# Order of the adjacency products within a tile: bank by bank, three products each

## The reference

```
x, adj                     # 10000 x 128, 10000 x 10000
u = max(layernorm(x), 0)
h = item_feat @ W_item.T + b_item        # 10000 x 128
b = u @ W_user.T + b_user
out = x + relu(adj @ h + b)
```

## Time and profile before

| | us |
|---|---|
| median of 3 runs | 1154.68 |
| lowest, highest | 1153.7, 1154.87 |
| the profiled execution, its own time | 1155.03 |
| its span, first to last instruction | 1153.5 |
| TensorE busy | 1132.1 |
| VectorE busy | 976.4 |
| ScalarE busy | 773.4 |

### The profile page before, as it was taken

The page is one execution under the profiler, slowest core; times in us unless marked ns, Lnnn a source line. Parts: engine busy times, 40 slices in busy tenths (PEclk is TensorE's granted clock), DMA queues, the critical chain, the costliest instruction groups (busy, mean ns, idle before and its releaser), DMA issues.

```text
span 1153.5 us, 14338 instructions
## 1 busy us (share of the span) xinstructions
PE 1132.1 (98%) x5078; PEld 925.8 (80%) x5078; DVE 976.4 (85%) x683; ACT 773.4 (67%) x502; POOL 20.3 (2%) x42
## 2 busy tenths in 40 slices
PE   6999999999999999999999999999999999999998
PEld 5888888878888888788888887888888878888886
DVE  5989988888888888898898888888888888888886
ACT  4766767667676666576667675766666657667663
POOL 0000000000000000000000000000000000000000
PEclk9999999999999999999999999999999999999999
DMA  9999999999999999999999998999999999999993
GB/s 355 397 400 359 352 364 372 347 362 345 376 372 360 367 365 392 365 370 368 355 367 362 385 379 338 376 362 373 357 371 380 381 331 378 376 358 353 364 387 120
DMA packets 62659, 416.38 MB, mean 361 GB/s; under 512 B 7644, under 2 KB 9124, under 8 KB 62608
## 3 DMA queue, kind: packets, MB, share of 16 engines
q1 hardware_dynamic: 59984, 406.38, 92.3%
q0 software_dynamic: 2624, 9.22, 2.3%
HBM read 410.45 MB, written 5.12 MB: 360 GB/s over the span
## 4 chain that ended last, share of the span: by engine, by line
PE 96%; DVE 1%; issue 1%; ACT 1%; DMA 1%; DVEq 0%; SPq 0%; ACTq 0%
PE acc L508 61%; PE acc L514 31%; PE spare L464 2%; PE acc L497 1%; DVE y L397 1%; PE spare L490 1%; PE spare L484 1%; ACT hi_ring L277 1%; DMA items<-in_item_t 1%; DVE lo_ring L340 0%; PE acc L525 0%; DVEq L94 0%; DVEq L427 0%; SPq L199 0%; SPq L188 0%
## 5 line engine op out<-in xcount | busy, mean ns | idle before, releaser
L340 DVE TENSOR_TENSOR lo_ring<-a_ring,hi_ring 128x2000 fp32r<-128x2000 f32 x390 | 871.3, 2241 | 152.8 <-ACT hi_ring L277 151.4
L277 ACT CAST hi_ring<-a_ring 128x2000 fp32r<-128x2000 f32 x390 | 729.0, 1869 | 360.6 <-PE acc L514 357.2
L508 PE MATMUL acc<-hi_ring,h_lo 128*128 128x500 f32 x1560 | 434.6, 399 | 5.5 <-DVE y L397 4.4
L508 PE MATMUL acc<-hi_ring,h_hi 128*128 128x500 f32 x1560 | 420.0, 391 | 0.0
L514 PE MATMUL acc<-lo_ring,h_hi 128*128 128x500 f32 x1560 | 419.1, 390 | 0.0
L508 PEld LDWEIGHTS acc<-hi_ring,h_lo 128*128 128x128 f32 x1560 | 289.5, 189 | 76.4 <-DVE y L397 12.4
L514 PEld LDWEIGHTS acc<-lo_ring,h_hi 128*128 128x128 f32 x1560 | 294.2, 189 | 62.1
L508 PEld LDWEIGHTS acc<-hi_ring,h_hi 128*128 128x128 f32 x1560 | 293.9, 188 | 61.7
L464 PE MATMUL spare<-wi,items 128*128 128x128 f32 x156 | 23.9, 294 | 10.5 <-DMA items<-in_item_t 8.7
L464 PEld LDWEIGHTS spare<-wi,items 128*128 128x128 f32 x156 | 23.0, 206 | 12.9 <-issue 6.8
L345 DVE TENSOR_TENSOR h_full<-spare,bi 128x384 f32<-128x384 f32 x26 | 14.3, 551 | 10.3 <-DMA bi<-in_b_item_rows 6.6
(11 more groups left out here) (29 smaller groups left out, 113.8 us busy)
## 6 DMA issues: line engine op xcount, KB each, us to landing
a_ring<-in_adj_tiles SPq DMA_DIRECT2D x390, 1000.0 KB, 6.9
rows<-in_x_rows POOLq DMA_DIRECT2D x20, 250.0 KB, 7.6
items<-in_item_t SPq DMA_DIRECT2D x12, 384.0 KB, 7.6
out_t<-y POOLq DMA_DIRECT2D x16, 250.0 KB, 5.3
out_t<-y SPq DMA_DIRECT2D x4, 250.0 KB, 2.2
a_rem<-in_adj_rem SPq DMA_DIRECT2D x20, 31.2 KB, 4.2
items<-in_item_t SPq DMA_DIRECT2D x2, 192.0 KB, 4.9
wi<-in_w_item_t SPq DMA_DIRECT2D x1, 64.0 KB, 1.8
```

What stands on the lines that cost most here:

```text
L277: nc.scalar.copy(hi_ring[:, r, :], a_ring[:, s, 0:GROUP_W]).then_inc(hi_written, 1)
L340: nc.vector.tensor_tensor(lo_ring[:, r, :], a_ring[:, s, 0:GROUP_W], hi_ring[:, r, :], ALU.subtract).then_inc(lo_written[s], 1)
L508: nc.tensor.matmul(acc[k][:, 0:BANK_W], h_part[:, c, :], hi_ring[:, r, k * BANK_W:(k + 1) * BANK_W], start=(c == 0 and h_part is h_lo), st ...
```

## The change

Within a tile, the loop over the banks is now the outer one. On each bank three products follow one another: `h_lo` with `hi_ring`, `h_hi` with `hi_ring`, `h_hi` with `lo_ring`. The wait for `lo_written` stands ahead of the third product of the tile, in place of the ninth. In a group's first tile the wait for `y_ready[k]` stands ahead of the first of the three products on bank k. The last product, which raises `chunk_used`, is the same one. The other engines' programs are unchanged.

```diff
                     pe.wait_ge(hi_written, g * CHUNKS + (c + 1))
-                    for h_part in (h_lo, h_hi):
-                        for k in range(ACC_BANKS):
-                            if c == 0 and h_part is h_lo:
-
-                                pe.wait_ge(y_ready[k], g + FREE)
-                            nc.tensor.matmul(acc[k][:, 0:BANK_W], h_part[:, c, :],
-                                             hi_ring[:, r, k * BANK_W:(k + 1) * BANK_W],
-                                             start=(c == 0 and h_part is h_lo), stop=False, skip_group_check=True)
-
-                    pe.wait_ge(lo_written[s], g * LOADS + (c // A_SLOTS + 1 + FREE))
                     for k in range(ACC_BANKS):
-                        last = nc.tensor.matmul(acc[k][:, 0:BANK_W], h_hi[:, c, :],
-                                                lo_ring[:, r, k * BANK_W:(k + 1) * BANK_W],
+                        cols = slice(k * BANK_W, (k + 1) * BANK_W)
+                        if c == 0:
+
+                            pe.wait_ge(y_ready[k], g + FREE)
+                        nc.tensor.matmul(acc[k][:, 0:BANK_W], h_lo[:, c, :], hi_ring[:, r, cols],
+                                         start=(c == 0), stop=False, skip_group_check=True)
+                        nc.tensor.matmul(acc[k][:, 0:BANK_W], h_hi[:, c, :], hi_ring[:, r, cols],
+                                         start=False, stop=False, skip_group_check=True)
+                        if k == 0:
+
+                            pe.wait_ge(lo_written[s], g * LOADS + (c // A_SLOTS + 1 + FREE))
+                        last = nc.tensor.matmul(acc[k][:, 0:BANK_W], h_hi[:, c, :], lo_ring[:, r, cols],
                                                 start=False, stop=False, skip_group_check=True)
                     last.then_inc(chunk_used[r], 1)
```

## The result

The changed kernel takes 1142.49 us, median of 4 runs (1141.89 to 1143.66), against 1154.78 of the kernel before in the same comparison: a ratio of 0.9897, with an interval of 0.9882 to 0.9912. The gain is 12.3 us. Forecast were 1148.0 us and a range down to 1145.6, so it is faster, as forecast, but by nearly twice as much, and outside of the range. The profiled execution took 1141.89 us (1155.03 before).

The account below looks back on a forecast made before the run. TensorE, busy 98% of the span, was taken to bound the kernel. From 1155.03 us, 4.0 for eviction waits and 3.0 for the clock were subtracted, giving 1148.0 us, with a range of 1145.6 to 1152.0.

Parts of the forecast that it names:

- (b): Group's first tile: second tile's load at 2.63 us, not 3.68; saves 1.0 us at each of four boundaries, 4.0 total.
- (c): Granted clock behind the group boundaries: full speed at all four, saving 3.0 us (bounds 0 and 3.0).
- Rival 1: Behind group boundaries the clock still falls: 1149.5 us with one fall, 1151.0 with two; chance 0.22.
- (d): Wait for low parts at each tile's third product, not ninth: 1.36 us earlier, tightest margin 0.33 us, cost 0.
- Rival 2: Low parts come late in 20 tiles at the layer norm, costing 4 us: 1152.0 us; chance 0.10.
- (a): Same 4680 products in another order: steady step stays 0.227 us, change zero; bounds 9.4 us penalty, 53 us gain.
- the sign: A steady tile not staying at 2.72 us would show (a) wrong; 0.006 us a tile is 2.3 us in all.
- the two bounds by the bank: Same-bank products: 0.003 us penalty for each of 3120, 9.4 us (rival's chance 0.12); or 53 us gain (chance 0.04).
- half a nanosecond on the step: Allowance in the range for a shorter step of all 4680 products: 0.0005 us each, 2.3 us.

Follow-up runs that it names:

- `shifted_old`: Both rings start 8 bytes into their buffers, in a kernel where only a group's first tile goes bank by bank; 1153.75 us in a single run.

## Why the prediction was right and wrong

- **(b), the group's first tile: right.** Forecast 2.63 us worked out (its terms give 2.62) and 1.0 saved, measured 2.61 and 1.07. The step with the wait for bank 1 is 0.02 longer than a plain one, the register step cost nothing that shows.
- **(c), the clock: right.** All four boundaries stay at full speed, 3.0 us in the profile. That it is 3.0 hangs on the two falls of the profiled execution; how many the other runs of the kernel before had isn't seen. Rival 1 has not come true in any profile with the new first tile.
- **(d), the low parts: right.** The tightest margin in the trace of the changed kernel is 0.23 us (a subtraction ends at 391.62, the load that needs it starts at 391.85), less than the 0.33 of the forecast, and no load waits for VectorE. Rival 2 falls.
- **(a), the step of a product: wrong, and it is the step that put the forecast out.** "In steady state I take the step of 0.227 us as it is." Late in a group it went from 0.2274 to 0.2259 us, and over all tiles that made 1.0 us in each of five groups, 5.0 in all. The prediction had named the sign, a steady tile that doesn't stay at 2.72, but held the term at zero. It set the two bounds by the bank, a penalty of 9.4 and a gain of 53 us; the runs show no price of the bank (215.90 and 216.92 us with the banks exchanged, as without), and a price of the order in which the moving columns are read, which hangs on the layout of the buffers and which no part of the forecast had. Within a tile of the kernel before, the steps go from 0.223 to 0.236 us, and the same ones come back every third tile. They were there to be read, and I had averaged them away.
- **The range** took in half a nanosecond on the step. The step moved by 1.1 ns on the mean of all products, and by 1.5 late in a group. The same rows had steady tiles from 2.72 to 2.73 us; 0.01 us on each of 390 tiles is 3.9 us, which would have been nearer, and still short of the 5.0.
- The sum with the measured terms: 1155.03 - 4.3 - 3.0 - 5.0 = 1142.7 us, against 1142.49 measured as the median.

## What to carry to other kernels

Where TensorE is the chain, a new accumulation that has to wait for its bank should be given all the work that it has for that bank before it asks for the next one. Here three of the four evictions then vanished behind products (the wait of 1.9 us for the first stays), and the clock stayed up. Before a gain of a few tenths of a per cent is put down to an order of instructions, shift the operands by a few bytes: here 8 to 64 bytes moved the time more than the order did. And where every step of a bound engine counts, read the steps one by one and by slot, not their mean.

## What was not expected of the hardware

- The step of a single-pass product with 500 moving columns depends on the layout of the buffers and on the order in which these columns come: on the mean of a tile 0.224 to 0.229 us (a twelfth of 2.69 us, the changed kernel's shortest steady tile, and of 2.75, the mean steady tile of `shifted_old`). The order keeps its price with one block of weights all through, with other banks, and with ScalarE and VectorE nearly idle. A pitch of 2048 bytes gave two fixed paces, 2.68 and 2.72 us for twelve.
- The point within the kernel's first tile from which its weight loads last 0.19 us in place of 0.33 differs between executions: the tile took 3.36 to 4.80 us in the 18 profiles. That puts about 1.4 us of chance on any single run of this kernel.
- Why the addresses matter, which buffer's place it is, and what selects one of the two paces at the pitch of 2048 bytes, stays open.
